# A graph layer with a mixture-of-experts FFN: chunks spread over two trips, their results kept in a DRAM list

## The reference, cut to what matters

```python
xn = layernorm(x)
agg = segment_sum(xn[src], dst) / max(degree, 1)
z = concat([xn, agg]) @ weight                      # 512 -> 256
x1 = x + z / norm(z) + bias
h = layernorm(x1)
probs = softmax(h @ gate_w + gate_b); e = argmax(probs)        # 8 experts
pos = running count of earlier rows of the same expert; kept = pos < 977
y = relu(h @ w1[e] + b1[e]) @ w2[e] + b2[e]         # 256 -> 1024 -> 256
out = x1 + nan_to_num(y * prob * kept)
```

## Time and profile before

| | before |
|---|---|
| median of 3 runs | 1421.02 us (1415.76 to 1421.20) |
| the profiled execution | 1421.57 us, span 1419.8 us |
| TensorE matmul, weight load busy | 1175.7 us (83%), 899.7 us (63%) |
| VectorE busy | 862.1 us (61%) |
| ScalarE busy | 474.8 us (33%) |
| GpSimd busy | 877.3 us (62%) |
| mean granted TensorE clock | 0.968 |

### The profile page before, as it was taken

How to read it: one execution, slowest core, us unless ns; L and a number is a source line. 1 busy time by engine, 2 the same in 40 slices (tenths; PEclk the granted TensorE clock), 3 DMA queues, 4 the chain that set the end, 5 groups by cost and what they waited for, 6 DMA issues and landing times.

```text
span 1419.8 us, 30155 instructions
## 1 busy us (share of the span) xinstructions
PE 1175.7 (83%) x5349; PEld 899.7 (63%) x5350; DVE 862.1 (61%) x3753; ACT 474.8 (33%) x1384; POOL 877.3 (62%) x933
## 2 busy tenths in 40 slices
PE   1076676889898989899989898989899999877885
PEld 0065565677777777777777777777767676654553
DVE  7645454666666666666666666666666666654443
ACT  3411112233333333333333333333333333343342
POOL 3167667777777777777777777777777777511101
PEclk9989888999999999999999999999999999988998
DMA  8686868443444443434343434343434443311111
GB/s 248 203 262 193 262 208 253 127 135 116 138 118 137 117 138 111 138 111 131 107 130 105 130 105 129 105 131 107 126 108 126 112 120 111 99 31 37 44 43 36
DMA packets 114562, 184.19 MB, mean 130 GB/s; under 512 B 21611, under 2 KB 85408, under 8 KB 114544
## 3 DMA queue, kind: packets, MB, share of 16 engines
q0 software_dynamic: 43424, 109.52, 27.9%
q1 hardware_dynamic: 71120, 74.48, 17.2%
HBM read 156.08 MB, written 36.09 MB: 135 GB/s over the span
## 4 chain that ended last, share of the span: by engine, by line
PE 45%; DVE 20%; DVEq 14%; issue 13%; DMA 6%; ACT 2%; SPq 1%; ACTq 0%; POOLq 0%; POOL 0%
PE ps_q L686 20%; PE ps_h L751 11%; PE ps_a L742 7%; DVE sel L994 5%; DVEq L1245 3%; PE ps_t L759 2%; DMA b_b<-in_L_ffn_b 2%; DVEq L851 2%; DMA ring<-xn_d,idx 2%; DMA out<-ys,node_i 2%; DVE row L1108 1%; DVE row L1112 1%; DVE bn L1114 1%; PE ps_b L770 1%; PE ps_q L691 1%
## 5 line engine op out<-in xcount | busy, mean ns | idle before, releaser
L458 POOL DMA_INDIRECT ring<-xn_d,idx x784 | 753.1, 961 | 305.3 <-issue 226.6
L686 PE MATMUL ps_q<-ring,sel 128*128 128x257 f32 (+1 forms) x1952 | 591.3, 406 | 121.2 <-DVE sel L994 88.5
L686 PEld LDWEIGHTS ps_q<-ring,sel 128*128 128x128 f32 x1952 | 342.2, 195 | 235.1 <-issue 172.3
L994 DVE SCALAR_TENSOR_TENSOR sel<-lane,block,dst_t 128x512 f32<-128x512 bf16 x245 | 184.1, 752 | 118.3 <-issue 82.3
L770 PE MATMUL ps_b<-w_sb,hid_t 128*128 x864 | 220.8, 386 | 12.6 <-ACT hid_t L605 8.1
L751 PE MATMUL ps_h<-w_sb,hid_t 128*128 x432 | 208.7, 610 | 5.6 <-ACT hid_t L584 5.6
L1003 DVE TENSOR_TENSOR acc<-acc,ps_q 128x257 f32 x245 | 103.3, 422 | 166.2 <-issue 128.2
L770 PEld LDWEIGHTS ps_b<-w_sb,hid_t 128*128 128x128 f32 x864 | 160.0, 190 | 38.4 <-issue 18.9
L472 POOL DMA_INDIRECT disp_d<-row,slot x53 | 54.7, 1031 | 124.0 <-DVEq L1065 120.3
L605 ACT ACTIVATE hid_t<-ps_t,b_t 128x128 f32<-128x128 f32 x432 | 117.2, 382 | 26.3 <-PE ps_t L759 26.3
L599 ACT ACTIVATE hid<-ps_h 128x512 f32<-128x512 f32 x108 | 64.5, 597 | 184.1 <-PE ps_h L751 184.1
(11 more groups left out here) (188 smaller groups left out, 1213.9 us busy)
## 6 DMA issues: line engine op xcount, KB each, us to landing
w_sb<-in_L_ffn_w SPq DMA_DIRECT2D x32, 512.0 KB
ring<-xn_d,idx POOLq DMA_INDIRECT x784, 2.8
disp_d<-hid SPq DMA_DIRECT2D x8, 1040.0 KB, 8.0
xs<-disp_d SPq DMA_DIRECT2D x55, 130.0 KB, 2.9
ys<-disp_d SPq DMA_DIRECT2D x55, 130.0 KB
b_b<-in_L_ffn_b SPq DMA_DIRECT2D x55, 128.0 KB
xb<-in_x SPq DMA_DIRECT2D x51, 128.0 KB
out<-row SPq DMA_DIRECT2D x51, 128.0 KB
```

The costliest lines, as they stand in the source:

```text
L458: pool.indirect_dma_start(ring[:, (k % 2) * TQ + j, 0:D], None, xn_d[:, :], bass.IndirectOffsetOnAxis(ap=idx[:, k * TQ + j:k * TQ + j + 1] ...
L686: mm = pe.matmul(ps[:, 0:width], sel[:, s, j, :], ring[:, (k % 2) * TQ + j, 0:width], start=(j == 0), stop=(j == TQ - 1), skip_group_check ...
L994: dve.scalar_tensor_tensor(out=sel[:, s, :, :], in0=lane[:, :].rearrange("p (j m) -> p j m", j=1).to_broadcast((P, TQ, P)), scalar=block0[ ...
```

## The change

- The main loop has 9 trips without a chunk and then 20 pairs of trips, with one chunk to a pair: 20 chunk slots where there were 41. In the first trip of a pair TensorE does the chunk's transposes and up, in the second the hidden transposes and down. VectorE does `result` in the first and `choose` in the second, each behind an If and no longer interleaved with `route` and `finish_row`. Chunks are numbered by u, no longer by the trip.
- `choose` lets an expert that has its 977 rows pass for its last, partial chunk too.
- The row is copied into a second tile `sent` beside `route`, and the dispatch sends that; new_row no longer waits for the dispatch.
- The results of the main loop's chunks are not scattered there. SyncE stores ys with its node numbers into a DRAM list res_d; in the closing trips 50 to 52 GpSimd loads 19 of these (the first is filler) into the ring's space, seven at a time, and scatters them into out.
- GpSimd issues the gathers of the next trip's first quad ahead of a trip's dispatch.
- A visit's extra one-column matmul becomes a bf16 one that doesn't read the ring, and only in a quad's last visit; the counts go to another PSUM bank and so no longer wait for the chunk's sum to be read.
- The fill of disp_d for the next trip is issued behind the dispatch. ScalarE's list is put into two-trip order likewise; in the closing trips it and TensorE's list are ordered anew (counts straight behind linear; the second half of down behind the row's transposes; the row's second norm behind the chunk's relus).

```diff
+PLAIN = C0 + 1
+PAIRS = (TRIPS - PLAIN) // 2
+SHIFT = TRIPS - (C0 + PAIRS)
...
+NREPLAY = PAIRS - 1
+NRB = 7
...
+    res_d = nc.dram_tensor("res_d", (PAIRS * P, ROW), FP32, kind="Internal").ap()
...
+        rbuf = ring[:, :, :].rearrange("p s c -> p (s c)")[:, 0:NRB * ROW].rearrange("p (s c) -> p s c", c=ROW)
+        sent = sb("sent", [P, ROW], FP32)
...
+            def keep_result(u):
+                sp.wait_ge(res_ready, chunks(u))
+                sp.dma_start(res_d[ds((u - C0) * P, P), :], ys[:, :]).then_inc(res_kept, 16)
...
+                if kept:
+                    sp.wait_ge(res_kept, 16 * chunks(u))
+                elif not isinstance(u, int):
+                    sp.wait_ge(res_out, 16 * (chunks(u) - PAIRS))
...
+                if u is not None:
+                    sp.wait_ge(code_ready, chunks(u))
+                    sp.wait_ge(xc_ready, chunks(u))
                     if prev:
                         sp.sem_inc(sp_turn, 1)
                         sp.wait_ge(disp_out, 16 * t)
                         sp.wait_ge(x1_out, 16 * t)
-                    load_xs(t + 1)
-                    load_ys(t)
+                    load_xs(u + 1)
+                    if kept:
+                        keep_result(u)
+                    load_ys(u, kept)
...
+            fill_block(0)
+            with sp.Fori(0, C0 - 1) as t:
+                trip(t, weights=True)
+                sp.wait_ge(disp_out, 16 * (t + 1))
+                sp.sem_inc(sp_turn, 1)
+                fill_block(t + 1)
+            trip(C0 - 1, weights=True)
+            trip(C0)
+            with sp.Fori(0, PAIRS) as i:
+                t = sp.snap(i * 2 + PLAIN)
                 trip(t)
+                trip(t + 1, i + C0, kept=True)
...
-                    disp_d[:, :], bass.IndirectOffsetOnAxis(ap=slot[0:rows, 0:1], axis=0), row[0:rows, :], None,
+                    disp_d[:, :], bass.IndirectOffsetOnAxis(ap=slot[0:rows, 0:1], axis=0), sent[0:rows, :], None,
...
+            def load_replay(r):
+                s, use = r % NRB, r // NRB
+                if use:
+                    pool.wait_ge(replay_out[s], 16 * use)
+                pool.dma_start(rbuf[:, s, :], res_d[(r + 1) * P:(r + 2) * P, :]).then_inc(replay_in[s], 16)
+            def replay(r):
+                s, use = r % NRB, r // NRB
+                pool.wait_ge(replay_in[s], 16 * (use + 1))
+                pool.sem_inc(pool_turn, 1)
+                pool.indirect_dma_start(
+                    out[:, :], bass.IndirectOffsetOnAxis(ap=rbuf[:, s, C_NODE:C_NODE + 1].bitcast(I32), axis=0),
+                    rbuf[:, s, 0:D], None, bounds_check=N - 1, oob_is_err=False).then_inc(replay_out[s], 16)
...
+            def trip(t, u=None, more=True, fill=False):
+                for k in range(1, QS):
+                    quad(t, k)
+                if more:
+                    quad(t + 1, 0)
+                scatters(t, u, fill=fill)
+            quad(0, 0)
             with pool.Fori(0, C0) as t:
-                trip(t, chunk=False)
-            with pool.Fori(C0, TRIPS) as t:
+                trip(t, fill=True)
+            trip(C0)
+            with pool.Fori(0, PAIRS - 1) as i:
+                t = pool.snap(i * 2 + PLAIN)
                 trip(t)
+                trip(t + 1)
+            trip(TRIPS - 2)
+            trip(TRIPS - 1, more=False)
+            pool.wait_ge(ring_free, 2 * TQ + NQ * TQ)
+            pool.wait_ge(res_kept, 16 * PAIRS)
+            for r in range(NRB):
+                load_replay(r)
...
+            for rows, batch in ((P, range(NRB)), (P, range(NRB, 2 * NRB)), (LAST, range(2 * NRB, NREPLAY))):
+                scatters(pool.snap(t_reg), pool.snap(t_reg) - SHIFT, rows=rows)
+                pool.reg_add(t_reg, t_reg, 1)
+                for r in batch:
+                    replay(r)
+                for r in batch:
+                    if r + NRB < NREPLAY:
+                        load_replay(r + NRB)
...
-                    width = AW if j < TQ - 1 else D
-                    mm = pe.matmul(ps[:, 0:width], sel[:, s, j, :], ring[:, (k % 2) * TQ + j, 0:width],
+                    mm = pe.matmul(ps[:, 0:AW], sel[:, s, j, :], ring[:, (k % 2) * TQ + j, 0:AW],
                                    start=(j == 0), stop=(j == TQ - 1), skip_group_check=True)
                     if final:
                         mm.then_inc(ring_free, 1)
                     if j == TQ - 1:
-                        mm = pe.matmul(ps[:, D:AW], sel[:, s, j, :], ring[:, (k % 2) * TQ + j, D:AW],
-                                       start=False, stop=True, skip_group_check=True)
+                        if final:
+                            mm = pe.matmul(ps[:, AW + 1:AW + 2], ones[:, :], ones[:, 0:1], start=True, stop=True,
+                                           skip_group_check=True)
                         mm.then_inc(visit_done, 1)
...
+                    pe.matmul(ps_q[1][:, C_CNT:C_CNT + EX], tri[0:rows, :], hot[0:rows, :], start=True, stop=True,
+                              skip_group_check=True)
+                    pe.matmul(ps_q[1][:, C_CNT + EX:C_CNT + 2 * EX], ones[0:rows, :], hot[0:rows, :],
+                              start=True, stop=True, skip_group_check=True).then_inc(count_ps, 1)
...
-                plan = [[steps((prev, gate), (chunk, load_expert)),
-                         steps(),
-                         steps((node, cat_transposes), (chunk, xc_transposes)),
+                plan = [[steps((prev, gate)),
+                         steps((first, load_expert)),
+                         steps((node, cat_transposes), (first, xc_transposes)),
                          steps()],
                         [steps((node, linear, 0)),
                          steps((node, linear, 1)),
-                         steps((chunk, up, 0)),
+                         steps((first, up, 0), (second, hid_transposes, 0)),
+                         steps((second, hid_transposes, 1))],
+                        [steps((prev, counts), (quads, load_quads)),
+                         steps((first, up, 1), (second, down, (0, 1))),
+                         steps((second, down, (2, 3))),
                          steps()],
-                        [steps((prev, counts), (chunk, up, 1), (quads, load_quads)),
-                         steps((chunk, hid_transposes, 0)),
-                         steps((chunk, hid_transposes, 1)),
-                         steps((chunk, down, (0, 1)))],
-                        [steps((chunk, down, (2, 3))),
-                         steps((chunk, down, (4, 5))),
-                         steps((chunk, down, (6, 7))),
+                        [steps((second, down, (4, 5))),
+                         steps((second, down, (6, 7))),
+                         steps(),
                          steps((node, xl_transposes), (quads, turn_quads))]]
-                for k in range(QS):
-                    if quads:
+                if quads:
+                    for k in range(QS):
                         quad(t, k, plan[k])
-                    else:
-                        for step in plan[k]:
-                            step()
+                else:
+                    steps((prev, gate), (node, cat_transposes), (chunk, load_expert), (node, linear, 0),
+                          (node, linear, 1), (prev, counts), (chunk, xc_transposes), (chunk, up, 0), (chunk, up, 1),
+                          (chunk, hid_transposes, 0), (chunk, hid_transposes, 1), (chunk, down, (0, 1, 2, 3)),
+                          (node, xl_transposes), (chunk, down, (4, 5, 6, 7)))()
...
-                dve.wait_ge(disp_out, 16 * (t + 1))
...
+            def send_copy(t):
+                def copy():
+                    if not isinstance(t, int):
+                        dve.wait_ge(disp_out, 16 * t)
+                    dve.tensor_copy(sent[:, :], row[:, :])
+                return [nothing, copy]
...
-                    dve.tensor_reduce(row[:, C_GATE:C_GATE + 1], g8[:, 2, :], AX, ALU.max)
+                    dve.tensor_reduce(sent[:, C_GATE:C_GATE + 1], g8[:, 2, :], AX, ALU.max)
...
+                    if whole:
+                        dve.tensor_scalar(full, seen[0:1, :], float(CAP), float(P - 1), ALU.is_ge, ALU.mult)
+                def top_up():
+                    dve.tensor_tensor(have, have, full, ALU.add)
...
+            def main_trip(t, half=None, u=None):
+                dve.load(next_regs, qtab[0:1, ds(t * QS + QS, QS), :])
+                dve.wait_ge(cat_ready, t + 1)
+                add_last(t, 0)
+                select_quad(t, 1)
+                chains(route(t), send_copy(t))
+                if half is not None:
+                    with dve.If(half > 0):
+                        dve.drain()
+                        chains(choose(u))
+                add_last(t, 1)
+                select_quad(t, 2)
+                chains(finish_row(t))
+                if half is not None:
+                    with dve.If(half < 1):
```

(83 more changed lines are left out.)

264 lines of the change are left out of this document (127 added, 137 removed).

## The result

The changed kernel takes **1508.5 us** (median of 4 runs, 1504.0 to 1510.3) against 1421.1 of the kernel before on the same chip: ratio **1.062 [1.058, 1.065]**, slower by 87 us. In a later comparison the two stood at 1509.0 and 1419.1, ratio 1.064 [1.061, 1.068]. The forecast was 1456, with 1505 as the upper end of the range. The sign, the place of the loss and the shorter end came out as forecast; the size did not.

A forecast was written before the change was run, and what follows sets the result against it. VectorE, working in order, was taken to fill the 23.8 us period. Terms 56 + 12 - 4 - 4 - 20.6 - 4 = +35 on 1421.57 gave 1457, stated as 1456; the 8 in 10 range was 1388 to 1505.

The forecast's parts named there:

- Bound: Main loop: VectorE, in order, fills the 23.8 us period; less matmul work could take away about 0.7 us a trip.
- Chunk-only trips: After the last node: two fewer trips with only a chunk, 7 instead of 9, at 10.3 us each: -20.6.
- Closing node trips: Three trips with a node behind the main loop: new_row no longer waits for the dispatch, 1.3 gained each: -4.
- Plain trips: Trips ahead of the chunk trips: one more, with gathers earlier in the rest: -4 (bounds -16, +4).
- GpSimd: Few irregular main-loop periods: copying the row to sent frees VectorE from waiting for that dispatch: -4; nothing in regular periods.
- The list: Closing trips: GpSimd's 19 replayed scatters and their loads are covered: 0, bound +8.
- First trip of a pair: VectorE without choosing: waits 1.5 for the counts, then finish_row and result one after the other: +1.7 us.
- Second trip: VectorE chooses alone after routing; next select waits for TensorE's visit with down, starting about 826.4 against 825.57: +0.8 us.
- Interleaving: VectorE in main trips, choose and result standing alone: mean +1.25, loop +0.2, dropped wait -0.05; over 40 trips +56.
- Clock: TensorE in main trips idles more, so its granted clock falls: 0.3 us a trip, +12.
- rival "clock": Half speed for most of both visits in VectorE's way, +1.7 in nearly every trip: +56 more, 1512; chance 0.13.

The follow-up runs named there:

- Order mended: Changed kernel with choose interleaved with route again and result with finish_row, each still once a pair: 1440.4 us, later 1443.9.
- the version with both repairs: Changed kernel with TensorE's register load back behind up's second visit, and choose and result interleaved with route and finish_row again: 1393.5 us, ratio 0.982 to the kernel before.
- the last comparison: Changed kernel, each repair alone (load, order) and both, rerun on a chip like the first: 1509.0, 1468.1, 1443.9 and 1393.5 us; kernel before 1419.1.
- the load mended: Changed kernel with TensorE's load of eight quad registers moved to the end of quad 1, behind the hidden transposes: 1462.7 us, later 1468.1.
- the top-up: Kernel before with only an eleventh step in choose, letting a full expert's short last chunk be taken: ratios 0.986, 0.981 and 0.984, all on slow chips.

## Why the prediction was wrong, step by step

- **Bound** (VectorE's order, matmuls free): right for TensorE's matmuls. Half of up and down away changed 0.1%. Yet "VectorE [...] fills the period" was too strong: VectorE's select, TensorE's visit and the next add wait for one another in a round, and a stop in TensorE's queue (the load) lengthened it.
- **Chunk-only trips**, -20.6: right (seven of 10.4; the rest after the closing trips -19.4).
- **Closing node trips**, -4: 77.9 to 70.2, -7.8, in the bounds. **Plain trips**, -4: +2.2, not to be told from nothing, as this stage takes 189.2 to 197.2 us in four traces with the same code there. **GpSimd** in irregular periods, -4: not seen apart, the pairs of trips 39 to 44 are irregular in the changed kernel too. **The list** at no cost: right.
- **First trip of a pair**, +1.7: +1.8 measured. A test cost less than my 0.25: the add is at 884.87 - 881.86 = 3.01 behind the start of routing, of which 2.91 is routing.
- **Second trip**, +0.8: the failed step. It reads that "The next select has to wait until the quad's visit with two pairs of down matmuls is through (822.5 + 8 x 0.44 = 826.0)". The counts came as forecast within 0.25 (863.77 - 855.35 = 8.42 against 823.25 - 814.60 = 8.65). But the matmuls behind them began 1.44 us late, and the visit ended so much later. I had moved up out of that slot of the plan in my count of TensorE's work and never asked what stood behind it in the queue: a load of registers of 1.96 us that up had covered. It costs 1.56 in each of 20 second trips, 31 us. Mending it gave 46 and 41, since half clock, told of below, then also costs time in five pairs only, instead of nine.
- **Interleaving**: I put the loss at 2.5 a pair, with 0.4 for the loop. Order mended gave 68 and 65 us, more than the 50 + 8. In pairs in which half clock, told of below, costs nothing, it is 52.1 - 49.1 = 3.0 a pair, 60 us: so this price, which the forecast had at 58 in all, was nearly right. The loop cost nothing that can be seen: it stands in the version with both repairs, whose pairs are 47.6.
- **Clock**, +12: right in size by luck, as it is not a slower pass in every trip. From the slot of a second trip to that of the first trip behind it the changed kernel takes 24.5 us in seven of its 20 pairs and 25.7 to 26.2 in nine (four are irregular). The first 4 us of four such stretches, the first and third of 24.5 and the other two of 26.2 and 26.1:

```profile
332.10:336.10 4.00, 3.29 (x15) 2.68 (x15) 0.92 (x4) 0.00 (x0) 2.16 (x3) 1.00 0.24 67
438.90:442.90 4.00, 3.86 (x10) 3.14 (x11) 0.56 (x3) 0.00 (x0) 1.34 (x2) 0.59 0.22 66
598.70:602.70 4.00, 3.29 (x15) 2.68 (x15) 0.92 (x4) 0.00 (x0) 2.15 (x3) 1.00 0.24 71
650.90:654.90 4.00, 3.89 (x10) 3.13 (x11) 0.52 (x3) 0.00 (x0) 1.31 (x2) 0.57 0.20 58
```

   At half clock (1.2 GHz instead of 2.4) ten matmuls fit where fifteen did. A stretch of it here costs 1.6; at other places it need not cost anything: the version with both repairs has one in every pair, and 16 of its 19 periods of a pair are 47.5 to 48.0 (the others 46.6, 46.7 and 49.3). Nine pairs are hit in the changed kernel: 14 us. Its first trips all have such a stretch too, so what it costs there, if anything, is not separated. In the traces of the last comparison this interval is longer (by 1.2 to 2.5, mostly 1.7) in ten regular pairs of the changed kernel, in five with the load mended, in 12 with the order mended and in one with both; the half clock then stands in the first 4 us behind the slot or 16 to 22 us behind it. The single repairs change that count by -5 and +2, both together by -9, six more than the two: 6 x 1.6 = 10 us beyond the sum, where 9 were measured; it is read from the traces, no run isolates it.

The sum again, with what was measured: order 60, load 31, clock 14 make 105 of the 108.4 in the main trips, and 27 come back at the end. The forecast had 64 for the main trips (56 + 12 - 4), and the load, which it put at nothing, is 31 of the 44 that it lacked. Two of its signs were off as well: from slot to slot the trips alternate between 27.7 and 24.5 or 26.1, not between 25.5 and 24.6, as the choice and the result both fall between the slot of a first trip and that of the second; and TensorE is busy 1041 us, not near 950, in part because matmuls at half clock take longer. The rival "clock" (1512) was near the time by chance: its mechanism, +1.7 in nearly every trip, is not what the periods show.

## What to carry to other kernels

Halving a piece of work is worth what it costs in the chain, not what it costs in busy time: here half the choices, results and chunk slots of the main loop were worth 4 us in 955 when nothing else was lost, and taking them apart to halve them exposed what was left. When a piece is moved out of an in-order queue, list what stands behind it and ask what it covered; a register load needs issued work ahead of it. Try a gain that can stand alone (the top-up, the closing trips) alone.

## What the hardware showed

- A load of eight registers from a table in SBUF holds TensorE's queue for 1.96 us, every time (1.947 to 1.978 in 49), and shows as "issue".
- A stretch of half clock costs 1.6 us if it falls in the first 4 us behind the slot of a second trip, and nothing that shows at the places where most pairs of the version with both repairs have theirs.
- On two of the four chips of the experiments the kernel before takes 19 to 21% longer, with stops between instructions: VectorE waits up to 3.0 us for its own sequencer ahead of a select, where it is 0.9 at most on the first chip. There the version with both repairs, which has 14% fewer instructions (26035 against 30155), is 4 to 6% faster than the kernel before, instead of 1.8%. What makes these stops was not tried.
